# A decoder layer on one core: sums and centring per weight and x^T in halves at the start, four slots for h and gate tiles and two down banks in the last FFNs, and new engine orders

## The reference, cut to what matters

```python
x = x + attn(layernorm(x))              # one head of 128: softmax(q k^T / sqrt(128)) v, masked head, w_o
x = x + xattn(layernorm(x), ctx, mask)  # relu(x W^T + b) against relu(ctx W^T + b), softmax, times ctx
x = x + ffn(layernorm(x))               # gate and up 256 -> 1024, silu(gate) * up, down 1024 -> 256
```

## Time and profile before

| | us |
|---|---|
| median of 3 runs (lowest, highest) | 376.03 (375.55, 376.86) |
| the profiled execution's own time | 375.11 |
| its span in the profile | 373.3 |
| PE busy | 362.1 |
| ACT busy | 318.2 |
| DVE busy | 314.7 |
| POOL busy | 293.2 |

### The profile page before, as it was taken

The page is one execution under the profiler, slowest core; times in us unless marked ns, Lnnn a source line. Parts: engine busy times, 40 slices in busy tenths (PEclk is TensorE's granted clock), DMA queues, the critical chain, the costliest instruction groups (busy, mean ns, idle before and its releaser), DMA issues.

```text
span 373.3 us, 7341 instructions
## 1 busy us (share of the span) xinstructions
PE 362.1 (97%) x2108; PEld 278.7 (75%) x2108; DVE 314.7 (84%) x914; ACT 318.2 (85%) x590; POOL 293.2 (79%) x421
## 2 busy tenths in 40 slices
PE   7999899999999999999999999999999999999995
PEld 4376688887788778877887778777887788767653
DVE  1955958875988899979999899998899889899995
ACT  3599977999899987999889885999779979979994
POOL 1551699828998997979969889698978698995884
PEclk9999999999999999999999999999999999999999
DMA  8657041132214345151345331803434112315343
GB/s 277 266 222 257 6 169 29 20 118 91 73 28 101 56 128 139 35 126 35 128 94 152 70 99 59 195 14 62 124 57 108 27 60 42 72 29 100 56 116 112
DMA packets 47591, 36.92 MB, mean 99 GB/s; under 512 B 39232, under 2 KB 40896, under 8 KB 47168
## 3 DMA queue, kind: packets, MB, share of 16 engines
q1 hardware_dynamic: 47552, 36.46, 36.1%
HBM read 23.07 MB, written 4.21 MB: 73 GB/s over the span
## 4 chain that ended last, share of the span: by engine, by line
PE 77%; ACT 6%; DVE 4%; DMA 4%; issue 4%; POOL 3%; SPq 1%; ACTq 0%; DVEq 0%; POOLq 0%
PE b_bank L1054 9%; PE b_bank L1056 9%; PE b_bank L1055 9%; PE d_bank L1285 6%; PE g_bank L1269 5%; PE a_bank L1054 5%; PE a_bank L1056 5%; PE a_bank L1055 5%; PE u_bank L1269 5%; PE b_bank L1197 3%; PE a_bank L1117 3%; DMA x_all<-in_x 2%; PE b_bank L1168 2%; DMA c_half<-c_half 2%; PE e_bank L1055 1%
## 5 line engine op out<-in xcount | busy, mean ns | idle before, releaser
L685 POOL TENSOR_TENSOR c_work<-c_work 128x512 f32<-128x512 f32 x48 | 61.6, 1291 | 8.1 <-DVE c_work L1519 5.3
L944 ACT ACTIVATE c_work<-g_bank,c_tanh_scale 128x512 f32<-128x512 f32 x52 | 35.9, 691 | 7.3 <-PE g_bank L1269 3.8
L732 POOL TENSOR_SCALAR c_work<-c_work,h_q 128x1024 f32<-128x1024 f32 x31 | 34.9, 1124 | 8.5 <-DVE h_q L1553 8.3
L1054 PE MATMUL b_bank<-ctx_hi,b_pT_hi 128*128 128x256 f32 x128 | 39.3, 307 | 0.0
L1519 DVE SCALAR_TENSOR_TENSOR c_work<-c_work,g_bank 128x512 f32<-128x512 f32 x50 | 33.8, 675 | 4.5 <-ACT c_work L944 4.5
L1055 PE MATMUL b_bank<-ctx_lo,b_pT_hi 128*128 128x256 f32 x128 | 36.1, 282 | 0.0
L1056 PE MATMUL b_bank<-ctx_hi,b_pT_lo 128*128 128x256 f32 x128 | 36.1, 282 | 0.0
L1285 PE MATMUL d_bank<-downT,c_half 128*128 128x256 bf16 x256 | 33.3, 273 | 2.0 <-ACT a_xT_raw L971 0.7
L1546 DVE TENSOR_REDUCE h_max<-c_work 128x1 f32<-128x1024 f32 x28 | 33.9, 1211 | 1.2 <-POOL c_work L685 1.0
L1269 PE MATMUL g_bank<-gateT,xqT 128*128 128x512 bf16 x112 | 33.6, 382 | 0.2 <-ACT c_work L932 0.2
L1269 PE MATMUL u_bank<-upT,xqT 128*128 128x512 bf16 x112 | 33.6, 381 | 0.0
(11 more groups left out here) (340 smaller groups left out, 1258.0 us busy)
## 6 DMA issues: line engine op xcount, KB each, us to landing
ctx_raw<-in_ctx SPq DMA_DIRECT2D x8, 512.0 KB, 4.2
x_all<-in_x SPq DMA_DIRECT2D x7, 512.0 KB, 3.6
a_xT_raw<-in_x_t SPq DMA_DIRECT2D x7, 512.0 KB, 5.7
ctxT_raw<-in_ctx_t SPq DMA_DIRECT2D x7, 512.0 KB, 4.5
out<-x_all SPq DMA_DIRECT2D x7, 512.0 KB, 2.8
r_bc<-r_rows SPq DMA_DIRECT2D x7, 256.0 KB, 4.3
c_work<-in_w_gate SPq DMA_DIRECT2D x1, 1024.0 KB, 9.9
c_work<-in_w_up SPq DMA_DIRECT2D x1, 1024.0 KB, 6.7
```

The lines of the kernel that those rows point to most:

```text
L685: pool.tensor_tensor(h[:, t % 2, half * HALF:(half + 1) * HALF], th[:, j % 2, :], up[:, j % 2, :], ALU.mult).then_inc(hs, 1)
L732: pool.tensor_scalar(h[:, t % 2, :], h[:, t % 2, :], h_q[:, t:t + 1], ROUND if n < LAST else ROUND_F16, ALU.mult, ALU.add).then_inc(h_roun ...
L944: act.activation(th[:, j % 2, :], gu_bank("g", j, n), ACT.Silu if (n, j) in SILU else ACT.Tanh, scale=c_tanh_scale[:, j // 2:j // 2 + 1]). ...
L1054: pe.matmul(dst, l_hi, r_hi, start=first, stop=False)
```

## The change

At the start the column sums, the centring and the wait for them are split by weight (Q, K, V), each with a PSUM bank of its own, and batch 0's x^T is loaded in two halves. In batches 6 and 7 the gate halves have four slots (`th4`), and h has one for each tile (`last_h`, two of them in `a_p`). In batch 7 the down products of tiles 1 and 3 go to `g_bank`. The five tables are written anew. The line numbers of the changed kernel are 13 to 21 higher than those of before.

```diff
-A_FRONT = """YP0/0 Q/0 K/0 V/0 S0/0 S1/0 VT/0 S2/0 S3/0 P0/0 YP1/0 P1/0 Q/1 P2/0 K/1 P3/0 V/1 H/0 YP0/1 VT/1 S0/1
+A_FRONT = """Q/0 K/0 V/0 S0/0 S1/0 VT/0 YP0/0 S2/0 S3/0 P0/0 YP1/0 P1/0 Q/1 P2/0 K/1 P3/0 V/1 H/0 YP0/1 VT/1 S0/1
...
 PE_ORDER = """
-    W.colsum/0 E.YP0/0 A.Q/0 A.K/0 A.V/0 W.r/0 A.S0/0 A.S1/0 E.YP1/0 A.VT/0 A.S2/0 A.S3/0 A.P0/0 A.P1/0 A.Q/1
+    W.sumQ/0 W.sumK/0 W.sumV/0 A.Q/0 A.K/0 A.V/0 W.r/0 E.YP0/0 A.S0/0 A.S1/0 A.VT/0 A.S2/0 A.S3/0 E.YP1/0 A.P0/0
...
 DVE_ORDER = """
-    W.centre/0 A.bn0/0 A.bn1/0 A.ag0/0 A.ag1/0 A.bn0/1 A.bn1/1 W.split/0 W.rs/0 A.K/0 W.lo/0 A.ag0/1 A.ag1/1
+    W.centreQ/0 W.centreK/0 A.bn0/0 A.bn1/0 A.ag0/0 A.ag1/0 W.centreV/0 W.split/0 W.rs/0 A.K/0 W.lo/0 W.wo0/0
...
 SP_ORDER = """
-    W.qkv/0 W.W/0 W.c/0 W.t/0 W.x0/0 W.x1/0 S.x/1 S.xT/1 F.gate/0 W.o/0 S.ctxT/1 S.mask/0 S.mask/1 S.rw/1 F.up/0
+    W.qkv/0 W.t0/0 W.t1/0 W.x0/0 W.x1/0 W.o/0 W.W/0 W.c/0 S.xT/1 S.ctxT/1 S.mask/0 S.x/1 F.gate/0 F.up/0
...
+        th4 = c_work[:, 0:2 * F].rearrange("p (c f) -> p c f", c=4)
+        last_h = [h[:, 0, :], h[:, 1, :]] + [a_p[:, 2 * i:2 * i + 2, :].rearrange("p t s -> p (t s)") for i in range(2)]
...
+        sum_bank = [b1_bank, d_bank, u_bank]
...
+        def h_tile(t, n):
+            return last_h[t] if n >= B - 2 else h[:, t % 2, :]
+
+        def gate_tile(j, n):
+            return th4[:, j % 4, :] if n >= B - 2 else th[:, j % 2, :]
+
+        def gate_slot_free(j, n):
+
+            if n < B - 2 or n == B - 2 and j < 4:
+                return h_ready(j - 2, n) if j > 1 and n < B - 2 else h_ready(2 * T - 2 + j % 2, n - 1)
+            return h_ready(j - 4, n) if j > 3 else h_ready(j + 4, n - 1)
...
+        def dn_bank(t, n):
+            return g_bank if n == LAST and t % 2 == 1 else d_bank
...
-                elif name == "t":
-                    sp.dma_start(xT_first[:, :, :], x_t[:, 0]).then_inc(xT0_loaded, 16)
+                elif name[0] == "t":
+                    c = int(name[1])
+                    sp.dma_start(xT_first[:, c, :], x_t[:, 0, c, :]).then_inc(xT0_loaded[c], 16)
...
                 elif name == "qkv":
-                    act.wait_ge(qkv_centred, 1)
+                    act.wait_ge(qkv_centred, 3)
...
-                if step == "Q":
-                    pe.wait_ge(qkv_centred, 1)
-                if step == "Q":
-                    pe.wait_ge(xT0_loaded, 16)
+                pe.wait_ge(qkv_centred, w + 1)
                 for c in range(DC):
+                    if step == "Q":
+                        pe.wait_ge(xT0_loaded[c], 16)
...
-                    if k > 0:
+                    if n == LAST and t == 1:
+                        pe.wait_ge(*g_read(2 * T - 2, LAST))
+                    elif n == LAST and t > 1:
+                        pe.wait_ge(*dn_read(t - 2, LAST))
+                    elif k > 0:
                         pe.wait_ge(*dn_read((k - 1) % T, (k - 1) // T))
...
-                        mm = pe.matmul(d_bank[:, 0:D], h_T[:, t % 2, f, :], downT[:, f, :], start=f == 0, stop=f == FC - 1)
+                        mm = pe.matmul(dn_bank(t, n)[:, 0:D], h_T[:, t % 2, f, :], downT[:, f, :], start=f == 0, stop=f == FC - 1)
...
-                        mm = pe.matmul(b1_bank[:, 0:3 * DH], ones[:, :], wqkv_raw[:, c, :, :].rearrange("p w d -> p (w d)"),
-                                       start=c == 0, stop=c == DC - 1)
+                        mm = pe.matmul(sum_bank[w][:, 0:DH], ones[:, :], wqkv_raw[:, c, w, :], start=c == 0, stop=c == DC - 1)
...
-                    if j % 2 == 0 and n == LAST and j > 2:
-                        dve.wait_ge(last_hT_filled, j - 2)
-                    elif j % 2 == 0:
+                    if n == LAST and j % 2 == 0:
+                        dve.wait_ge(hqs, T * (n - 1) + j // 2 + 1)
+                    elif j == 4:
+                        dve.wait_ge(a_filled, a_rank("P3", LAST))
+                    elif j % 2 == 0 and j < 4:
                         dve.wait_ge(hqs, T * n + j // 2 - 1)
...
-            def centre_qkv():
-                dve.wait_ge(qkv_sums, 1)
+            def centre(w):
+                dve.wait_ge(qkv_sums, w + 1)
                 for c in range(DC):
-                    raw = wqkv_raw[:, c, :, :].rearrange("p w d -> p (w d)")
-                    last = dve.scalar_tensor_tensor(raw, b1_bank[:, 0:3 * DH], -1.0 / D, raw, ALU.mult, ALU.add)
+                    raw = wqkv_raw[:, c, w, :]
+                    last = dve.scalar_tensor_tensor(raw, sum_bank[w][:, 0:DH], -1.0 / D, raw, ALU.mult, ALU.add)
```

More of the change, by code:

```diff
@@ L90 @@
-    A.Y1/2 C.g0/0 E.YP1/3 C.u0/0 A.Q/3 C.u1/0 C.g1/0 B.S0/1 B.S1/1 A.K/3 B.P0/1 C.g2/0 B.S2/1 C.u2/0 A.V/3
-    B.P1/1 B.O0/1 C.u3/0 C.g3/0 B.S3/1 B.P2/1 C.g4/0 C.u4/0 B.O1/1 C.g5/0 A.VT/3 A.S0/3 C.u5/0 E.YP0/4 B.P3/1
-    B.O2/1 C.g6/0 B.O3/1 C.u6/0 C.DN0/0 B.XT0/2 E.YP1/4 B.XT1/2 C.g7/0 C.u7/0 A.S1/3 A.P0/3 B.XP0/2 B.XP1/2
-    A.S2/3 A.P1/3 C.u0/1 C.g0/1 A.S3/3 C.DN1/0 C.u1/1 B.S0/2 C.g1/1 B.S1/2 C.DN2/0 B.P0/2 B.S2/2 C.DN3/0 C.g2/1
-    C.u2/1 B.P1/2 B.O0/2 C.g3/1 C.u3/1 A.P2/3 A.P3/3 B.S3/2 B.P2/2 C.g4/1 C.u4/1 A.H/3 B.O1/2 C.g5/1 A.Y0/3
@@ new lines @@
+    A.V/3 B.P1/1 C.u3/0 C.g3/0 B.O0/1 B.S3/1 B.P2/1 C.g4/0 C.u4/0 E.YP0/4 C.g5/0 B.O1/1 C.u5/0 B.P3/1 B.O2/1
+    A.VT/3 A.S0/3 B.O3/1 C.g6/0 C.u6/0 E.YP1/4 B.XT0/2 B.XT1/2 C.g7/0 C.DN0/0 C.u7/0 A.S1/3 A.P0/3 B.XP0/2
+    B.XP1/2 A.S2/3 C.DN1/0 C.u0/1 C.g0/1 A.P1/3 A.S3/3 B.S0/2 B.S1/2 C.g1/1 C.u1/1 B.P0/2 B.S2/2 C.DN2/0 C.g2/1
+    C.u2/1 C.DN3/0 B.P1/2 B.O0/2 A.P2/3 A.P3/3 C.g3/1 C.u3/1 B.S3/2 B.P2/2 C.g4/1 A.H/3 B.O1/2 B.P3/2 C.u4/1
+    A.Y0/3 A.Y1/3 C.g5/1 C.u5/1 A.Q/4 A.K/4 C.u6/1 B.O2/2 B.O3/2 C.DN0/1 C.g6/1 B.XT0/3 B.XT1/3 A.V/4 E.YP0/5
@@ new lines @@
+    C.u2/3 B.P1/4 B.O0/4 C.g3/3 B.S3/4 A.P2/5 A.P3/5 C.u3/3 B.P2/4 B.O1/4 C.u4/3 A.H/5 C.g4/3 E.YP0/6 A.Y0/5
+    A.Y1/5 B.P3/4 C.u5/3 C.g5/3 B.O2/4 A.Q/6 A.K/6 B.O3/4 C.g6/3 C.u6/3 A.V/6 B.XT0/5 B.XT1/5 E.YP1/6 C.u7/3
+    C.g7/3 A.VT/6 A.S0/6 B.XP0/5 C.u0/4 C.g0/4 B.XP1/5 C.DN0/3 C.g1/4 C.u1/4 C.DN1/3 A.S1/6 A.P0/6 B.S0/5 B.S1/5
+    C.g2/4 A.S2/6 A.P1/6 B.P0/5 C.DN2/3 C.u2/4 A.S3/6 B.S2/5 C.u3/4 C.DN3/3 C.g3/4 B.P1/5 B.O0/5 A.P2/6 A.P3/6
+    C.u4/4 C.g4/4 B.S3/5 B.P2/5 A.H/6 B.O1/5 C.g5/4 C.u5/4 A.Y0/6 A.Y1/6 B.P3/5 B.O2/5 C.g6/4 A.Q/7 A.K/7 C.u6/4
@@ new lines @@
+    B.O3/5 A.V/7 C.DN0/4 C.u7/4 A.VT/7 A.S0/7 B.XT0/6 B.XT1/6 E.YP0/7 C.g7/4 A.S1/7 A.P0/7 B.XP0/6 B.XP1/6
+    A.S2/7 A.P1/7 C.g0/5 C.u0/5 C.DN1/4 A.S3/7 C.g1/5 B.S0/6 B.S1/6 A.P2/7 C.u1/5 A.P3/7 B.P0/6 B.S2/6 A.H/7
+    C.g2/5 B.P1/6 B.O0/6 C.u2/5 A.Y0/7 A.Y1/7 C.u3/5 C.g3/5 B.S3/6 B.P2/6 E.YP1/7 C.g4/5 B.O1/6 C.u4/5 B.P3/6
+    B.O2/6 C.u5/5 C.g5/5 C.DN2/4 B.O3/6 C.u6/5 C.g6/5 C.DN3/4 B.XT0/7 B.XT1/7 C.u7/5 C.g7/5 C.DN0/5 B.XP0/7
+    B.XP1/7 C.g0/6 C.u0/6 C.u1/6 C.g1/6 C.DN1/5 B.S0/7 B.S1/7 C.g2/6 B.P0/7 B.S2/7 C.u2/6 C.g3/6 B.P1/7 C.u3/6
```

310 lines of the change are left out of this document (150 added, 160 removed).

## The result

The changed kernel takes 372.56 us (372.06 to 373.97, 4 runs), the kernel before in the same comparison 375.96 (375.55 to 376.86); the ratio is 0.991, 95% interval 0.9882 to 0.9939. It is faster by 0.9%, further than the 374.6 forecast and 0.14 us outside the stated range of 372.7 to 377.3. The profiled execution took 372.06 with a span of 370.1, 3.2 less than the span before.

The account below looks back on a forecast made before the run. PE was taken to bound the kernel, busy 362.1 of 373.3 us, leaving only idle time to win. The terms -0.1 + 1.0 + 0.3 - 1.9 - 0.7 = -1.4 gave 374.6 from 376.03, range 372.7 to 377.3.

Parts of the forecast that it names:

- the dense middle: 45 to 250 us, PE always busy: sign steps ahead of ReLU pairs on ACT cost +0.3, between 0 and 2.4.
- The front: Start of the program: earlier W.rs is spent on E.YP0/0, which lost its cover; -0.1, between -0.3 and +0.1.
- the rival on the loads: At the start, x lands sooner, S0/0 starts 2.0 earlier and the time is 372.7; chance 0.15.
- Batch 1: ACT's moved sums delay exponentials and A.H/1, so PE waits more: +1.0, between 0 and +2.4.
- The late waits: PE's late single waits of 0.2, 0.4 and 0.7 all go: -1.9, between -1.3 and -2.0.
- 0.2 per hole: Added to each of the three late waits, since a hole costs somewhat more than the idle time shown; a choice.
- The tail: Last stretch: h slot wait gone, u7/7 earlier, C.DN2/7 moved; -0.7, between -2.35 and +0.5.
- +0.5: In the tail, the cost of C.DN2/7 standing between hT3 and C.DN3/7.
- -0.55: In the tail, DVE's wait for the slot of h goes with a tile of h each.
- -0.65: In the tail, the gain from u7/7 ahead of hT1 and C.DN0/7, with the transposes.
- The rival on the tail: At the end, all 2.35 of PE's holes go instead of 0.7, giving 373.0; chance 0.13.

Follow-up runs that it names:

- loads_back: The changed kernel with W and ctx^T loaded again ahead of batch 0's x^T and x; 372.28 us, ratio 0.991.
- best_b: As best_a, with one more weight sum ahead of A.H/0 on ACT in place of the two x^T roundings of batch 2; 372.35 us, ratio 0.9924.
- dn2_first: The changed kernel with C.DN2/7 ahead of hT3 on PE, as before; 373.57 us, ratio 0.9956.
- act_old: The changed kernel with ACT's order of before for batch 1's sums, YP0/1 pair, batch 2's x^T and the second exponential; 374.72 us, ratio 0.9976.
- old_front: The changed kernel with the front's old order of loads, centrings, statistics and E.YP0/0, sums still split and x^T in halves; 374.54 us, ratio 0.998.
- rs_first: The kernel before with W.rs/0 and A.K/0 ahead of W.split/0 on DVE; 374.63 us against 375.26, ratio 0.9987.
- one_bank: The changed kernel with all down products of batch 7 in d_bank again; 373.83 us, ratio 0.9964.
- two_slots: The changed kernel with the two slots of before for h in batch 7; 376.04 us, ratio 1.0022.
- best_a: As stats_late, with A.H/6 and B.P2/5 also ahead of batch 7's statistics on DVE; 371.67 us, ratio 0.9901.
- best_d: The changed kernel with batch 1's x loaded ahead of its x^T and ctx^T, and ACT's W.r/0 ahead of E.ctxT/1 and A.xT1/1; 372.06 us, ratio 0.9913.
- stats_late: The changed kernel with A.V/0 ahead of batch 1's statistics on DVE; 371.50 us, ratio 0.9893.

## Why the prediction was wrong, step by step

That PE's work and the dense middle stay, and that only idle time can be won, was right: 0.93 of lead at A.H/1, 1.01 at A.VT/7, where the prediction had a loss of 0.3.

**The front, "-0.1", failed in size and in what carries it.** Measured: -0.9. By waits it is plain: PE's work up to A.Q/1 is the same in both, and its waits there, behind the column sums, were 1.73 and 0.65 before and 0.48 and 1.01 after, 0.89 less. The chain was right in kind: V's product waited for V's centring behind the statistics, and E.YP0/0 stood between W.r and S0. Its prices were not: x was there by 7.22 instead of 7.9, a product takes 1.72 instead of 1.9, and W.rs, entered at 1.75 from the earlier trace rows, took 0.69. S0/0 came at 14.48, where I had 16.7 and the rival on the loads 14.6. Then half of these 2.1 was lost on what no step named: A.V/0 behind statistics that wait for x of batch 1. What carries the rest is settled only in part. Load order, split sums and E.YP0/0's place, undone one at a time or two together, cost 0 to 0.2 of lead each, no more than the scatter. W.rs clear of POOL gave the kernel before 0.6 us timed, with an interval that takes in no change. The 372.7 of the rival on the loads is near the measured 372.56 by luck: it keeps 1.9 of the front where 0.9 came, and without the sooner loads (loads_back) the time is the same. More can't be said, since the loads alone move PE's start on E.YP0/0 by 1.4 between two executions.

**Batch 1, "+1.0", was wrong, and this is the largest term.** Measured: 0.0. I added a chain of rounded prices on from 19 us and compared its end with a row. From A.H/0's rounding, which I put at 33.6 to 34 and which came at 32.24, to the end of the last exponential I had 9.4; it took 8.67 (32.24 to 40.91), and before 8.53 (33.17 to 41.70). The difference of the two orders is smaller. Ahead of A.H/0's rounding two sums (2.5) are out and the YP0/1 pair (1.3) and the two roundings of x^T (1.2) in, which is nothing: from the rounding of K/1 it took 6.66 before and 6.65 after, where I had 0.4 to 0.8 more. Behind it two sums are in (2.3, 33.22 to 35.52) and the pair (1.3) and the mask (0.5) out, E.ctxT/2 in both: 0.5, of which 0.14 came. And the hole is a round trip between PE and ACT that no sum stands in (best_b).

**The late waits, "-1.9", were sized too high.** All three waits went. Those of 0.39 and 0.67 gave 0.8 by B.P0/7, less than their own sum, so the 0.2 per hole that I added on top isn't to be seen. The one of 0.20, at 281.81 ahead of A.VT/7, was paid back by new ones of 0.21 at 137.2 and 0.16 at 254.9. Where the rest went isn't traced.

**The tail, "-0.7", was sized too low, with a term of the wrong sign.** C.DN2/7 behind hT3 was entered as +0.5; dn2_first shows that the other order loses 1.3 from hT2 to the last down product (0.24 and 0.92 of new holes). The slots and u7/7's place, entered at -0.55 and -0.65, show only 0.2 of lead by C.DN1/7. The 1.5 came behind it, where the kernel before waited for the read of `d_bank` and then 0.36 for ACT's copy:

```profile
367.40 1.03 PE L1285 MATMUL d_bank<-downT,c_half 128*128 128x256 bf16 x8 [0.70 <-ACT a_xT_raw L971]
```

The sum had no term for that read, which the second bank takes away. The rival on the tail had all 2.35 of holes going: PE's last 10 us are dense, but waits of 0.49 and 0.56 remain at 352.1 and 355.7. The finish grew by 0.3.

Front and batch 1 together were off by 1.8 of the 2.0 us between 374.6 and 372.56; the other three errors (middle -0.4, late waits +1.1, tail with the finish -0.7) cancel, which is luck.

## What to carry to other kernels

When an order changes, price the difference of the two orders between two steps that both have, and not the new chain from the start. Before a lead is entered, look down the same queue for the next step that waits for a load: a lead ends where an engine waits for data that come no sooner. And two tables written together are undone together, or the experiment measures a mismatch (act_old, old_front).

## What the runs showed of the hardware

W.rs, a product of two SBUF tensors on DVE, took 0.68 or 0.69 in nineteen traces and 1.75 in the kernel before. There it began behind a POOL instruction of the same kind:

```profile
13.63 3.08 POOL L623 TENSOR_TENSOR a_xT_lo<-a_xT_raw,a_xT_hi 128x512 fp32r<-128x512 f32 x2 [0.61 <-ACT a_xT_hi L826]
13.82 1.75 DVE L1348 TENSOR_TENSOR vT<-ident,a_rstd 128x512 f32<-128x512 f32 x1
```

In rs_first the split, which then fell beside POOL, took 1.45 where it had 0.94. The Trainium skill, "SBUF — State Buffer", section "SBUF: two separate sides", says that VectorE with two SBUF inputs and GpSimd take a shared pair of ports as a lock, and that the one that comes second waits for the whole instruction. The trace agrees: POOL's second instruction began at 14.99, and 14.99 plus 0.69 is 15.68, near the 15.57 at which W.rs ended. I had read 1.75 as the step's own price. The step W.lo shows it without an edit, in two traces with the same tables up to there. In one_bank POOL began first:

```profile
12.39 1.27 POOL L643 TENSOR_TENSOR a_xT_lo<-a_xT_raw,a_xT_hi 128x512 fp32r<-128x512 f32 x1 [1.58 <-ACT a_xT_hi L844]
...
12.62 1.59 DVE L1627 TENSOR_TENSOR wt_lo<-xqT,wt_hi 128x512 fp32r<-128x512 f32 x1
```

In the changed kernel DVE did, and POOL took the 1.59:

```profile
12.27 0.68 DVE L1631 TENSOR_TENSOR wt_lo<-xqT,wt_hi 128x512 fp32r<-128x512 f32 x1
...
12.49 1.59 POOL L643 TENSOR_TENSOR a_xT_lo<-a_xT_raw,a_xT_hi 128x512 fp32r<-128x512 f32 x1 [2.02 <-ACT a_xT_hi L844]
```

A long wait of PE can cost more than itself. In act_old PE stood still for 2.17 ahead of 41.40 and in two_slots for 2.66 ahead of 18.18; in both the granted clock then went from 1.00 to 0.50, the lower of its two levels (1.2 and 2.4 GHz), for about 3 us. In two_slots the same work from A.VT/0 to A.VT/1 took 16.41, in the changed kernel 14.68. In the profiled execution of old_front the clock stayed at 1.00 after a wait of 2.40, so such a wait doesn't always do it.

The load of x of batch 7 waits on SP, by the kernel's own semaphore, until a store of 512 KB has landed, since it takes the stored slot. That store took 2.6 us from issue to landing in the changed kernel and in best_a, 4.4 in best_d and 5.1 in stats_late; what makes it long isn't shown. So a store's landing, and not only PE's lead, sets when x of batch 7 can come.
